# The filling turns of a pipelined attention stage: bias tables behind the first roots on GpSimd, two buffers for statistics and tokens, another order on ScalarE

## What is computed

```python
h = _layernorm(x) * (1 + ca) + sa
x = x + ga * attention(h)
h = _layernorm(x) * (1 + cb) + sb
x = x + gb * experts(h)
```

```python
for i, o in enumerate(OFFSETS):
    lg = (q * shift(k, o)).sum(-1) * inv * (1 + qs[..., i]) + pos_bias[i]
p = softmax(logits)
out = sum(p[..., i] * shift(v, o)) * if_gain
return (out * sigmoid(x @ gate_w.T + gate_b)) @ out_w.T + out_b
```

## Time and profile before

| what | us |
|---|---|
| three runs: lowest, median, highest | 1223.79, 1228.4, 1243.09 |
| the profiled execution, its own time | 1224.34 |
| its span, first to last instruction | 1222.6 |
| span of `attention1` in it | 749.8 to 1083.9 |
| its filling turns, to the first work of turn 0 on DVE | 749.8 to 799 |

### The profile page before, as it was taken

The page is one execution under the profiler, slowest core; times in us unless marked ns, Lnnn a source line. Parts: engine busy times, 40 slices in busy tenths (PEclk is TensorE's granted clock), DMA queues, the critical chain, the costliest instruction groups (busy, mean ns, idle before and its releaser), DMA issues. The chain is left out here.

```text
span 1222.6 us, 24942 instructions
## 1 busy us (share of the span) xinstructions
PE 1054.5 (86%) x9293; PEld 619.5 (51%) x9293; DVE 806.5 (66%) x1863; ACT 584.7 (48%) x1125; POOL 536.2 (44%) x674
## 2 busy tenths in 40 slices
PE   3768789999999999999999995699999999754398
PEld 2324344444444444444444442498887888744352
DVE  4446567777866877667555753498899998636433
ACT  1124455555455555454554442566666775421142
POOL 4535645567547655543454445232122221014525
PEclk9998799999999999999999998578899999865599
DMA  4695455445354445442333230533233322022233
GB/s 129 177 192 107 95 129 118 110 109 144 67 130 123 106 106 112 107 105 64 121 106 94 74 106 6 172 94 106 62 99 107 96 84 89 2 75 82 86 100 102
DMA packets 89559, 125.14 MB, mean 102 GB/s; under 512 B 10377, under 2 KB 58301, under 8 KB 85729
## 3 DMA queue, kind: packets, MB, share of 16 engines
q1 hardware_dynamic: 68032, 85.98, 28.2%
q10 hardware_dynamic: 19872, 34.61, 9.4%
q0 software_dynamic: 1536, 2.96, 0.8%
HBM read 91.58 MB, written 31.73 MB: 101 GB/s over the span
## 5 line engine op out<-in xcount | busy, mean ns | idle before, releaser
L543 POOL TENSOR_TENSOR a_gw<-a_half,a_wb 128x512 f32<-128x512 f32 x128 | 162.5, 1269 | 247.0 <-ACT a_half L630 210.7
L585 ACT ACTIVATE a_pr<-ps 128x512 f32<-128x512 f32 x192 | 114.3, 597 | 127.2 <-PE ps L714 125.0
L1003 DVE TENSOR_REDUCE a_nmax<-ps 128x2 f32<-128x512 f32 (+1 forms) x192 | 130.9, 686 | 64.1 <-PE ps L725 63.9
L849 PE MATMUL ps<-a_e_hT,e_wg 128*128 128x512 f32 x272 | 146.9, 622 | 0.3 <-ACT a_th L632 0.3
L1150 DVE SCALAR_TENSOR_TENSOR a_up<-a_th,ps 128x512 f32<-128x512 f32 x136 | 92.8, 682 | 81.9 <-PE ps L862 78.8
L871 PE MATMUL ps<-a_hm,e_wd 128*128 128x512 f32 x272 | 143.5, 609 | 0.6 <-DVE a_hm L1162 0.6
L862 PE MATMUL ps<-a_e_hT,e_wu 128*128 128x512 f32 x272 | 144.0, 611 | 0.0
L630 ACT ACTIVATE a_half<-ps 128x512 f32<-128x512 f32 x136 | 80.9, 595 | 105.4 <-PE ps L849 105.4
L1162 DVE TENSOR_TENSOR a_hm<-a_up,a_gw 128x512 f32<-128x512 f32 x128 | 111.8, 873 | 1.9 <-POOL a_gw L543 0.5
L681 PE MATMUL ps<-a_mask,identb 128*128 128x256 bf16 (+1 forms) x192 | 64.5, 336 | 27.7 <-DVE a_nmax L1003 9.8
L514 POOL TENSOR_SCALAR_AFFINE_SELECT a_pr<-a_pr 128x512 f32<-128x512 f32 x128 | 86.7, 701 | 0.0
(11 more groups left out here) (303 smaller groups left out, 2164.0 us busy)
## 6 DMA issues: line engine op xcount, KB each, us to landing
a_wb<-e_wT_d ACTq DMA_DIRECT2D x128, 256.0 KB, 3.3
a_gw<-a_gd_d SPq DMA_DIRECT2D x16, 1024.0 KB, 4.9
a_qs<-a_terms_d SPq DMA_DIRECT2D x32, 384.0 KB, 5.3
a_ks<-a_terms_d SPq DMA_DIRECT2D x32, 384.0 KB, 6.6
a_gd_d<-a_gc SPq DMA_DIRECT2D x64, 132.0 KB, 2.3
a_terms_d<-a_parts SPq DMA_DIRECT2D x32, 192.0 KB, 2.2
a_terms_d<-a_parts SPq DMA_DIRECT2D x32, 128.0 KB, 2.6
a_terms_d<-a_parts SPq DMA_DIRECT2D x32, 64.0 KB, 2.7
```

The source lines that it names most:

```text
L543: nc.gpsimd.tensor_tensor(gw[:, par], half[:, par], wb[:, (u - 1) % RING], ALU.mult).then_inc(weighted, 1)
L585: nc.scalar.activation(dst, src, ACT.Exp).then_inc(exp_done, 1)
L849: nc.tensor.matmul(ps[:, G_BANK, :], wg[:, u, :], e_hT[:, c.k % 2, :], start=True, stop=True).then_inc(gates_full, 1)
L1003: nc.vector.tensor_reduce(dst, src, AX_X, ALU.max, negate=True).then_inc(m_read, 1)
```

## The change

Three things, all in `attention1`:

1. POOL clears `vb` and builds the bias tables in a step `tables` that runs in turn -2, after `products` of batch 0, instead of ahead of its list.
2. `stat`, `mv`, `rstd`, `shift`, `y`, `ca` and `sa` get two buffers, and the holds on them go from the batch before to the batch before that.
3. In the turns -4 to -1 POOL and ACT run other lists (`first`): on POOL `rstd_of` comes ahead of `products`, on ACT `normalise` comes ahead of `modulate`.

```diff
-        ga, ca, sa = sb("ga", [P, 2]), sb("ca", [P, 1]), sb("sa", [P, 1])
-        stat, mv, rstd = sb("stat", [P, TB, 6]), sb("mv", [P, TB, 2]), sb("rstd", [P, TB])
-        y = sb("y", [P, TB, D])
+        ga, ca, sa = sb("ga", [P, 2]), sb("ca", [P, 2]), sb("sa", [P, 2])
+        stat, mv, rstd = sb("stat", [P, 2, TB, 6]), sb("mv", [P, 2, TB, 2]), sb("rstd", [P, 2, TB])
+        y = sb("y", [P, 2, TB, D])
...
-        def run(eng, order):
+        def run(eng, order, first=None):
...
-                for stage, step in order:
+                for stage, step in first if first and b.k < 0 else order:
...
-            nc.gpsimd.memset(vb[:], 0.0).then_inc(cleared, 1)
-            pool.wait_ge(cleared, 1)
-            nc.gpsimd.memset(vb[0:WIN, :, 0::2, HD], 1.0).then_inc(cleared, 1)
-            nc.gpsimd.memset(vb[WIN:P, :, 1::2, HD], 1.0).then_inc(cleared, 1)
-            pool.wait_ge(cleared, 3)
...
-            biases(0)
-            biases(1).then_inc(cleared, 1)
+            def tables(b):
+                if b.k != 2:
+                    return
+                nc.gpsimd.memset(vb[:], 0.0).then_inc(cleared, 1)
+                pool.wait_ge(cleared, 1)
+                nc.gpsimd.memset(vb[0:WIN, :, 0::2, HD], 1.0).then_inc(cleared, 1)
+                nc.gpsimd.memset(vb[WIN:P, :, 1::2, HD], 1.0).then_inc(cleared, 1)
+                pool.wait_ge(cleared, 3)
+                biases(0)
+                biases(1).then_inc(cleared, 1)

             def rstd_of(b):
                 pool.wait_ge(stats_done, b.x + 1)
-                hold(pool, y_done, 1, b, 0)
+                hold(pool, y_done, 1, b, -1)
...
-            run(pool, [("S", products), ("L", rstd_of), ("T", next_root)])
+            run(pool, [("S", products), ("L", rstd_of), ("T", next_root)],
+                [("L", rstd_of), ("S", products), ("L", tables)])
...
             run(act, [("T", take_p(0)), ("A", modulate), ("T", take_p(1)), ("T", take_p(2)), ("T", take_p(3)),
                       ("A", queries_keys), ("A", factors), ("T", gate), ("X", exps(0)), ("X", exps(1)), ("D", projected),
-                      ("L", normalise), ("T", gate_factors), ("X", values), ("T", next_normalise)])
+                      ("L", normalise), ("T", gate_factors), ("X", values), ("T", next_normalise)],
+                [("L", normalise), ("A", modulate), ("A", queries_keys), ("A", factors), ("X", exps(0)), ("X", exps(1)),
+                 ("X", values)])
...
             def statistics(b):
-                hold(v, stats_done, 1, b, 0)
+                hold(v, stats_done, 1, b, -1)
...
             def moments(b):
                 v.wait_ge(dve_a, b.x * TB + TB)
-                hold(v, hT_done, 1, b, 0)
-                hold(v, rstd_done, 4, b, 0)
+                hold(v, hT_done, 1, b, -1)
+                hold(v, rstd_done, 4, b, -4)
```

More of the change, by code:

```diff
@@ L1738, in attention1 @@
         gd = s["a1_gd"]
-        shift, pause = sb("shift", [P, TB]), sb("pause", [P, 1])
+        shift, pause = sb("shift", [P, 2, TB]), sb("pause", [P, 1])
         none = sb("none", [P, TB])
@@ L1820, in biases @@
                                                aw["early"][:, k].unsqueeze(2).to_broadcast([P, FAR_N, H]), ALU.add)
-            biases(0)
-            biases(1).then_inc(cleared, 1)
+            def tables(b):
[8 more added lines that the diff above has]
+                biases(1).then_inc(cleared, 1)
             def rstd_of(b):
                 pool.wait_ge(stats_done, b.x + 1)
-                hold(pool, y_done, 1, b, 0)
-                nc.gpsimd.tensor_tensor(rstd[:], mv[:, :, 1], s["eps"][:, 0:TB], ALU.add).then_inc(rstd_done, 1)
+                hold(pool, y_done, 1, b, -1)
+                nc.gpsimd.tensor_tensor(rstd[:, b.k % 2], mv[:, b.k % 2, :, 1], s["eps"][:, 0:TB], ALU.add).then_inc(rstd_done, 1)
                 pool.wait_ge(rstd_done, b.x * 4 + 1)
-                nc.gpsimd.tensor_tensor(rstd[:], rstd[:], s["pm5"][:, 0:TB], ALU.pow).then_inc(rstd_done, 1)
+                nc.gpsimd.tensor_tensor(rstd[:, b.k % 2], rstd[:, b.k % 2], s["pm5"][:, 0:TB], ALU.pow).then_inc(rstd_done, 1)
                 pool.wait_ge(rstd_done, b.x * 4 + 2)
-                nc.gpsimd.tensor_tensor(shift[:], mv[:, :, 0], rstd[:], ALU.mult).then_inc(rstd_done, 1)
+                nc.gpsimd.tensor_tensor(shift[:, b.k % 2], mv[:, b.k % 2, :, 0], rstd[:, b.k % 2], ALU.mult).then_inc(rstd_done, 1)
                 pool.wait_ge(rstd_done, b.x * 4 + 3)
-                nc.gpsimd.tensor_tensor(shift[:], none[:], shift[:], ALU.subtract).then_inc(rstd_done, 1)
+                nc.gpsimd.tensor_tensor(shift[:, b.k % 2], none[:], shift[:, b.k % 2], ALU.subtract).then_inc(rstd_done, 1)
             def products(b):
@@ L1873, in modulate @@
                 act.wait_ge(a_full, b.x * 2 + 1)
-                nc.scalar.activation(hT[:, b.k % 4, PAD:], ps[:, 4, 0:L], ACT.Identity, bias=sa[:], scale=ca[:]
+                nc.scalar.activation(hT[:, b.k % 4, PAD:], ps[:, 4, 0:L], ACT.Identity, bias=sa[:, b.k % 2:b.k % 2 + 1], scale=ca[:, b.k % 2:b.k % 2 + 1]
                                      ).then_inc(hT_done, 1)
@@ L1880, in normalise @@
                     at = bass.ds(b.x * TB + k, 1)
-                    a = nc.scalar.activation(y[:, k, :], x[:, at, :].rearrange("p a d -> p (a d)"), ACT.Identity,
-                                             bias=shift[:, k:k + 1], scale=rstd[:, k:k + 1])
+                    a = nc.scalar.activation(y[:, b.k % 2, k, :], x[:, at, :].rearrange("p a d -> p (a d)"), ACT.Identity,
+                                             bias=shift[:, b.k % 2, k:k + 1], scale=rstd[:, b.k % 2, k:k + 1])
                 a.then_inc(y_done, 1)
@@ L1983, in turn_tokens @@
                 for k in range(TB):
-                    mm = nc.tensor.transpose(ps[:, 4, k * P:(k + 1) * P], y[:, k, :], ident[:])
+                    mm = nc.tensor.transpose(ps[:, 4, k * P:(k + 1) * P], y[:, b.k % 2, k, :], ident[:])
                 mm.then_inc(a_full, 1)
@@ L2134, in statistics @@
             def statistics(b):
-                hold(v, stats_done, 1, b, 0)
+                hold(v, stats_done, 1, b, -1)
                 nc.vector.memset(pause[:], 0.0)
                 for k in range(TB):
-                    nc.vector.bn_stats(stat[:, k, :], x[:, bass.ds(b.x * TB + k, 1), :].rearrange("p a d -> p (a d)")
+                    nc.vector.bn_stats(stat[:, b.k % 2, k, :], x[:, bass.ds(b.x * TB + k, 1), :].rearrange("p a d -> p (a d)")
                                        ).then_inc(dve_a, 1)
@@ L2142, in moments @@
                 v.wait_ge(dve_a, b.x * TB + TB)
-                hold(v, hT_done, 1, b, 0)
-                hold(v, rstd_done, 4, b, 0)
-                nc.vector.tensor_copy(ca[:], modT[:, 1, 1, bass.ds(b.x, 1)])
-                nc.vector.tensor_copy(sa[:], modT[:, 1, 0, bass.ds(b.x, 1)])
+                hold(v, hT_done, 1, b, -1)
+                hold(v, rstd_done, 4, b, -4)
+                nc.vector.tensor_copy(ca[:, b.k % 2:b.k % 2 + 1], modT[:, 1, 1, bass.ds(b.x, 1)])
+                nc.vector.tensor_copy(sa[:, b.k % 2:b.k % 2 + 1], modT[:, 1, 0, bass.ds(b.x, 1)])
                 for k in range(TB):
-                    n = nc.vector.bn_aggr(mv[:, k, :], stat[:, k, :])
+                    n = nc.vector.bn_aggr(mv[:, b.k % 2, k, :], stat[:, b.k % 2, k, :])
                 n.then_inc(stats_done, 1)
```

## The result

The changed kernel takes 1236.84 us in the median of 20 runs (1228.93 to 1246.58), the kernel before 1231.7 us (20 runs, 1217.98 to 1244.82). The ratio is 1.0069, with a 95% interval of 1.0036 to 1.0103: a small loss, within 2% of no change. The profiled execution has a span of 1241.2 us against 1222.6, but little of these 18.6 us belongs to the change, as the stages show.

What follows compares the result with a forecast made beforehand. PE bounds the kernel almost everywhere, but the filling is a chain of waits. 1224.34 - 6.85 (gain) + 10.7 (new wait, relief included) = 1228.2 us, plus half of 4.1 for the median: 1230, 8 in 10 within 1220 to 1241.

Steps and rivals of the forecast that it cites:

- parts 1 and 2: Filling: tables behind the first roots, ACT's new order; first modulate 6.0 us early, second modulate 6.85 us early.
- part 3: Turn -1: ACT's normalise of batch 3 waits for DVE's moments, behind stage X; costs about 10.7 us.
- ACT idle some 10 us: Sign of being right: ACT idle this long ahead of a normalise at 787 to 788, released by POOL's shift.
- The relief: Turn -1: POOL's products no longer run beside add_bias; 2.15 us off, bounds nothing and 2.15.
- side reading: DVE's near logits, which read PSUM, are not slowed by the shared port: 3.64 us both times.
- The sum: Whole kernel: 1224.34 - 6.85 + 10.7 = 1228.2 us, with turn 0 3.85 us late; median forecast 1230.
- The loop: Turns from 0 on: old lists, two buffers change nothing there, no DMA or instruction added.
- dealt anew: Rival: the loop starting at another moment moves the total some 6 us either way, 1222 to 1234; chance 0.13.
- The rival on PE's clock: PE's wait in the filling delays the clock's rise by 5 us of work, costing 2.5 us: 1230.7; chance 0.08.
- the level: Median against profiled execution: half of the 4.1 us seen over three runs added, taking 1228.2 to 1230.
- The likeliest case's own range: Total time if the forecast case holds: 1224 to 1236 us; that case's chance 0.64.
- the wide range: Total time, 8 in 10: 1220 to 1241 us, from near the whole gain to dearer rivals on a high median.

Runs made afterwards that it cites:

- tables alone: Kernel before with only the tables step moved behind the root of batch 2 in turn -2; filling 43.01 us, ratios 0.9902 and 0.9983 in two blocks.
- lists alone: Changed kernel with the tables back at the head of POOL's queue, new lists and buffers kept; filling 59.71 us, ratio 1.0102.
- moments first: Changed kernel with a filling list for DVE in which moments follow statistics, ahead of stage X; filling 47.52 us, ratio 0.9987.

## Why the prediction was right

**The gain** of parts 1 and 2 was put at 6.85 us for the second modulate and measured 7.13. Half of the 0.28 is already in the first modulate, 6.13 early where 6.0 was worked out; the other half is the normalise ahead of the second, which took 0.77 us of ACT's time, not 0.9. The tables alone gain 6.6, where 6.7 was worked out.

**The wait** of part 3 was put at 10.7 us. The third modulate went from 7.13 early to 3.56 late: 10.69. The run with the lists alone and the run with moments first show that it is this wait, and where it hangs. One sign was misstated: "ACT idle some 10 us" is what the order adds. ACT already stood 7.18 us ahead of the third modulate before, and the row after has 17.80, 10.62 more.

**The relief** was taken at its upper bound, 2.15 us, and is 2.15. Its side reading, that products don't slow the near logits, was taken from two pairs beside which no products ran. Where they do, in turn 0 of the kernel before, it holds nearly: 3.72 us for the pair at 812.44, beside products at 813.57.

**The sum**, +3.85 us in the filling, measured +3.54; the 0.3 is the second modulate's.

**The loop.** In the profiles it took 284.7 and 280.6 us for the kernel before (from `add_bias` of turn 0 to POOL's first memset of the experts), 283.7, 287.1 and 290.3 for the changed one, and 280.2 to 291.2 over all kernels, with the same lists. That is the rival "dealt anew", which is an addition to each case rather than a case; it was put at 6 us either way. Its reason, another moment at which the loop starts, isn't needed: the two profiles of the kernel before have the same filling and differ by 4.1 us in the loop. The rival on PE's clock did not happen: the clock was at 0.50 when PE resumed, as it had been since 762, and rose in the second of these stretches, in PE's windows and transposes of turn 0, after PE had been busy from 805 on (the clock is the third number from the end):

```profile
801.90:814.90 13.00, 10.80 (x138) 9.00 (x135) 6.18 (x7) 5.83 (x11) 2.43 (x2) 0.50 0.40 125
814.90:817.90 3.00, 3.00 (x20) 2.90 (x19) 2.97 (x3) 2.72 (x6) 1.68 (x1) 0.78 0.00 0
```

In finer stretches the rise is at 816.2, 3.1 us behind the start of turn 0's `add_bias`; before it was at 803.8, 4.4 us behind. The wait did not delay it.

**What was off** is the level. I added 2 us to the profiled execution for the median; over 20 runs the kernel before stands at 1231.7, 7.4 above its profiled execution. With 7.4 and +3.5 the sum is 1235.2, the measured median 1236.8. Of the 6.8 us between the forecast of 1230 and the median, 5.4 are this level. The likeliest case's own range, 1224 to 1236, missed the median by 0.8 us; the wide range held it because it had been widened for a run of 1243. The mechanism and the size of the filling were worked out, the total was right by that width. Three runs were too few to take a level from.

## What to carry to other kernels

A step moved ahead on an in-order engine must be followed to its producer's place in the producer's own list: two buffers free the data, not the place in the queue. Here `normalise` went to the head of ACT's turn while the moments it needs stayed behind the longest stage of DVE's, and that ate the whole gain of an edit which by itself is worth 6.6 us. Move both ends or neither. Here both gave fillings of 47.52 and 43.54 us, neither (the tables alone) 43.01, and the shortest, 41.3, came from moving the step only in the turns in which its producer was early enough. And time a change of a few us by a stretch between two fixed instructions of the profile: fillings repeated within 0.06 us where the means of one kernel against the kernel before moved by 6. Such a stretch doesn't tell what happens behind it, so the total has the last word where the runs can resolve it.

## What was not expected of the hardware

Very small GpSimd operations stand still beside VectorE operations with two SBUF inputs. An addition on 128x2 elements took 1.17 us instead of 0.20 and a power 1.65 instead of 0.70, while DVE's pair kept its 2.49 us; beside GpSimd's large products it is the pair that grows to 4.67, and the products grow from 3.03 to 4.1. Who loses seems to hang on who is already running: the products of the kernel before start at 784.05, ahead of the pair at 784.64, and the slow addition at 778.54, behind the pair at 778.38. No run here swaps that order alone.

PE's granted clock falls in the middle of dense work. In the trace of before, behind the rise, with PE busy for all of both stretches:

```profile
812.00:815.00 3.00, 3.00 (x47) 2.86 (x46) 3.00 (x3) 1.53 (x6) 1.43 (x1) 0.84 0.52 86
815.00:818.00 3.00, 3.00 (x17) 3.00 (x18) 1.96 (x7) 1.23 (x2) 1.64 (x2) 0.59 0.79 315
```

There turn 0 lasts 819.01 - 799.38 = 19.6 us. In the first profile of the changed kernel the clock is at full speed in the same part of the turn, 12.65 to 18.65 us behind its `add_bias`, and the turn lasts 830.99 - 813.05 = 17.9:

```profile
825.70:828.70 3.00, 3.00 (x50) 2.90 (x50) 3.00 (x3) 1.48 (x4) 1.63 (x1) 1.00 0.49 107
828.70:831.70 3.00, 3.00 (x30) 2.94 (x29) 3.00 (x9) 1.32 (x4) 1.44 (x2) 1.00 0.64 261
```

This is not the change. Of the 14 profiles, six have the clock at full speed from 12 to 18 us behind turn 0's `add_bias`, and their turn 0 lasts 17.92 to 17.96 us; eight have it at 0.50 to 0.65 in the last 3 of these 6 us, and theirs lasts 19.39 to 19.86. Profiles of the changed kernel are in both groups (17.94, 17.92 and 19.80), and so are those of the tables alone (17.92 and 19.52). That such dips make up the spread of the loops, 280 to 291 us with the same lists, is likely but was not added up, and why they come where they do was not tried. Two stages that no edit touches moved as much: the attention began between 749.8 and 760 us, and the experts behind it took 138.5 to 147.3 us.
